# Two normalisation groups with GpSimd's reciprocal roots, and products without a reader in TensorE's waits

## What is computed

```python
for each of the two layers:
    h = _layernorm(x) * (1 + ca) + sa
    x = x + ga * attention(h)      # layer 0: convolutions, linear attention; layer 1: causal attention
    h = _layernorm(x) * (1 + cb) + sb
    x = x + gb * ffn(h)            # layer 0: 16 experts, top 4; layer 1: the stack below

def _L1_ffn_ref(x, ...):           # the windowed stack, DEPTH = 6, on 4 batches
    for i in range(DEPTH):
        x = attn_layer(shift_tokens(x), Wqkv[i], q_scale[i], k_scale[i], Wo[i]) + x
        x = ffn_layer(shift_tokens(x), ln_g[i], ln_b[i], W1[i], b1[i], W2[i], b2[i]) + x

def ffn_layer(x, g, bln, W1, b1, W2, b2):
    xn = layernorm(x) * g + bln
    a, gate = split(xn @ W1 + b1)  # 341 columns each
    return a * gelu(gate) @ W2 + b2
```

## Time and profile before

| what | value |
|---|---|
| median of 3 runs | 2385.68 us (2383.3 to 2389.93) |
| the profiled execution | 2394.28 us |
| its span, first to last instruction | 2392.7 us |
| PE busy | 2209.9 us (92%) |
| DVE, ACT, POOL busy | 1786.4, 1730.1, 1238.2 us |
| mean granted TensorE clock | 0.963 of full speed |

### The profile page before, as it was taken

One profiled execution on the slowest core, in us unless ns is written; L12 is line 12 of the kernel. 1 busy time (PEld: TensorE's weight loads), 2 busy tenths in 40 slices (PEclk: granted clock), 3 DMA queues, 4 the chain that ended last, 5 costly groups with the idle time before them and its releaser, 6 DMA issues.

```text
span 2392.7 us, 82108 instructions
## 1 busy us (share of the span) xinstructions
PE 2209.9 (92%) x33332; PEld 1573.3 (66%) x33332; DVE 1786.4 (75%) x3567; ACT 1730.1 (72%) x3982; POOL 1238.2 (52%) x2002
## 2 busy tenths in 40 slices
PE   6799679999976799999999999999999999999986
PEld 3478358888855566666766666666666676666662
DVE  3477377777777778888888888888888888888851
ACT  2255468888855578888888887887877888878870
POOL 0177010000000677777777777777777777776750
PEclk9899889999997899999999999999999999999996
DMA  2000022211102111112211111111111221111010
GB/s 89 10 1 2 2 96 76 80 64 70 71 2 82 28 51 53 49 49 60 58 51 51 45 53 53 51 47 55 53 51 51 56 61 45 58 53 54 25 40 22
DMA packets 40968, 117.74 MB, mean 49 GB/s; under 512 B 7953, under 2 KB 13393, under 8 KB 37777
## 3 DMA queue, kind: packets, MB, share of 16 engines
q1 hardware_dynamic: 40592, 112.49, 15.9%
HBM read 50.48 MB, written 2.23 MB: 22 GB/s over the span
## 4 chain that ended last, share of the span: by engine, by line
PE 50%; DVE 8%; ACT 5%; issue 3%; POOL 1%; DMA 0%; ACTq 0%; SPq 0%; POOLq 0%; DVEq 0%
PE w_psP L1784 13%; PE w_psT L1793 7%; PE w_psF L1728 7%; PE w_psS L1811 6%; PE w_psO L1840 6%; PE w_psF L1750 4%; PE w_psF L1754 3%; PE w_psT L1822 3%; ACT w_pb L1892 2%; DVE w_nrm L1957 2%; PE w_psS L1802 2%; ACT w_kT L1884 1%; DVE w_psP L1950 1%; DVE w_bb L1949 1%; DVE w_ab L1952 1%
## 5 line engine op out<-in xcount | busy, mean ns | idle before, releaser
L2054 POOL TENSOR_TENSOR w_ab<-w_ab,w_nrm 128x512 f32<-128x512 f32 x384 | 396.4, 1054 | 8.4 <-POOL w_nrm L84 8.4
L1892 ACT ACTIVATE w_pb<-w_psS,w_mx 128x64 f32<-128x64 f32 x1536 | 350.7, 347 | 2.6 <-PE w_psT L1822 1.0
L1784 PE MATMUL w_psP<-w_hi,w_xh 128*128 128x512 f32 x576 | 319.7, 555 | 33.5 <-DVE w_ab L1952 19.2
L2070 POOL TENSOR_TENSOR w_pb<-w_pb,w_sm 128x512 f32<-128x512 f32 x192 | 200.5, 1044 | 222.4 <-DVE w_sm L1970 222.4
L1957 DVE TENSOR_REDUCE w_nrm<-w_sq 128x8 f32<-128x512 f32 x384 | 251.9, 672 | 66.1 <-ACT w_sq L1867 66.1
L2046 POOL TENSOR_TENSOR w_ab<-w_ab,w_bb 128x512 f32<-128x512 f32 x192 | 245.5, 1279 | 87.3 <-DVE w_bb L1945 81.9
L1867 ACT ACTIVATE w_sq<-w_psP 128x512 f32<-128x512 f32 x384 | 235.6, 614 | 74.3 <-PE w_psP L1784 41.3
L1793 PE MATMUL w_psT<-tables_all,w_ab 128*128 128x128 f32 x1536 | 241.4, 280 | 7.3 <-POOL w_ab L2054 1.9
L1197 DVE TENSOR_TENSOR e_glo<-e_hh,e_ghi 128x512 fp32r<-128x512 f32 x256 | 169.5, 686 | 92.9 <-ACT e_ghi L1151 92.8
L1784 PE MATMUL w_psP<-w_lo,w_xh 128*128 128x512 f32 x576 | 229.5, 398 | 0.0
L1784 PE MATMUL w_psP<-w_hi,w_xl 128*128 128x512 f32 x576 | 229.1, 398 | 0.0
(11 more groups left out here) (294 smaller groups left out, 5387.0 us busy)
## 6 DMA issues: line engine op xcount, KB each, us to landing
X<-tables_layer SPq DMA_DIRECT2D x48, 384.0 KB, 3.7
X<-w_v SPq DMA_DIRECT2D x48, 384.0 KB, 3.6
e_gb<-gate_rows SPq DMA_DIRECT2D x16, 1024.0 KB, 4.8
e_raw<-in_w_moe SPq DMA_DIRECT2D x32, 256.0 KB, 5.2
w_raw<-in_w_qkv SPq DMA_DIRECT2D x20, 384.0 KB, 4.0
X<-tables_layer SPq DMA_DIRECT2D x48, 128.0 KB, 3.9
w_o<-in_w_o SPq DMA_DIRECT2D x6, 512.0 KB, 5.6
w_xs<-H SPq DMA_DIRECT2D x24, 128.0 KB, 2.2
```

The source lines that it names most:

```text
L1784: last = pe.matmul(psP[u % 2][:, :], x[r % 2][:, tt], w[:, layer % 2, ww], start=(n == 0), stop=(n == len(terms) - 1))
L1892: last = act.activation(pb[k % 2][:, n, :], psS[:, j, KEYS * q:KEYS * (q + 1)], ACT.Exp, bias=mx[:, n:n + 1])
L2054: pool.tensor_tensor(a, a, nrm[k // 2][:, 1, 8 * (i % 8):8 * (i % 8) + 8].unsqueeze(2).to_broadcast([128, 8, DH]), ALU.mult).then_inc(s["n ...
L2070: pool.tensor_tensor(p, p, sm[k % 2][:, :].unsqueeze(2).to_broadcast([128, PAIRS, KEYS]), ALU.mult).then_inc(s["pn"], 1)
```

## The change

It adds a helper `keep_busy`, which issues float32 products whose result nobody reads, and calls it in three places: in `adaln`, 4 products of 512 columns between the psX and the back transposes, into the bank `psB[3]`; in the first round, one product of 256 columns into `psF` ahead of each of the 24 units P and V, before their waits; in the last round's tail, 3 products ahead of `tr`, 5 ahead of `back`, one ahead of each of the other seven matmul steps, into `psP[0]`. Second, `adaln` takes statistics and aggregates in two groups of two batches; the roots and the shift of the first group are worked out by GpSimd (`rsqrt_simple` with 12 operations, and two for the shift), those of the second by VectorE, whose shift falls away.

```diff
--- before.py
+++ after.py
@@ -232,7 +232,7 @@
 
     nc = c.nc
     c.passed = c.sem("passed", keep=True)
-    c.adaln_sems = [c.sem("n_s_" + k, keep=True) for k in ("tr", "yn_act", "yn_dve", "back", "rs", "dve")]
+    c.adaln_sems = [c.sem("n_s_" + k, keep=True) for k in ("tr", "yn_act", "yn_dve", "back", "rs", "dve", "pool")]
     c.mods = c.sb("mods", [D, 2, 6, NB], keep=True)
     c.ident_bf = c.sb("ident_bf", [D, D], BF16, keep=True)
     c.band_bf = c.sb("band_bf", [D, 2, 256], BF16, keep=True)
@@ -294,6 +294,13 @@
             ch.link(dve.tensor_copy(c.band_bf[:, :, :], c.band[:, :, :]))
 
 
+def keep_busy(pe, bank, weights, moving, count):
+
+
+    for _ in range(count):
+        pe.matmul(bank, weights, moving, start=True, stop=True, skip_group_check=True)
+
+
 def adaln(c, layer, part, loads=None, yn=None):
 
 
@@ -307,7 +314,8 @@
     shift = c.sb(n + "shift", [128, NT])
     psX = [c.ps(n + f"psX{b}") for b in range(NB)]
     psB = [c.ps(n + f"psB{b}") for b in range(NB)]
-    s_tr, s_yn_act, s_yn_dve, s_bk, s_rs, s_ch = c.adaln_sems
+    s_tr, s_yn_act, s_yn_dve, s_bk, s_rs, s_ch, s_pool = c.adaln_sems
+    early, late = slice(0, NT // 2), slice(NT // 2, NT)
     call = 2 * layer + part
     gain = lambda b: c.mods[:, layer, 3 * part + 1, b:b + 1]
     add = lambda b: c.mods[:, layer, 3 * part, b:b + 1]
@@ -324,6 +332,7 @@
                     at = b * N + 128 * t
                     last = pe.transpose(psX[b][:, 128 * t:128 * t + 128], c.X[:, at:at + 128], c.ident[:, :])
                 last.then_inc(s_tr, 1)
+            keep_busy(pe, psB[3][:, :], c.ident[:, :], c.X[:, 0:N], 4)
             for b in (0, 2, 1, 3):
                 if b < 2:
                     pe.wait_ge(s_yn_act, call * 2 + b + 1)
@@ -349,17 +358,16 @@
         @block.vector
         def _(dve):
             ch = Chain(dve, s_ch, 2 * NT + 9, call)
-            for b in range(NB):
-                dve.wait_ge(s_tr, call * NB + b + 1)
-                for t in range(TILES):
-                    mark = ch.inc(dve.bn_stats(stats[:, b * TILES + t, :], psX[b][:, 128 * t:128 * t + 128]))
-            ch.wait(mark)
-            for k in range(NT):
-                mark = ch.inc(dve.bn_aggr(mv[:, k, :], stats[:, k, :]))
-            ch.wait(mark)
-            rsqrt(dve, ch, rs[:, 0, :], mv[:, :, 1], rs[:, 1, :], rs[:, 2, :], 1e-5, ALU.add)
-            dve.scalar_tensor_tensor(out=shift[:, :], in0=mv[:, :, 0], scalar=-1.0, in1=rs[:, 0, :], op0=ALU.mult,
-                                     op1=ALU.mult).then_inc(s_rs, 1)
+            for half in range(2):
+                for b in range(2 * half, 2 * half + 2):
+                    dve.wait_ge(s_tr, call * NB + b + 1)
+                    for t in range(TILES):
+                        mark = ch.inc(dve.bn_stats(stats[:, b * TILES + t, :], psX[b][:, 128 * t:128 * t + 128]))
+                ch.wait(mark)
+                for k in range(2 * TILES * half, 2 * TILES * (half + 1)):
+                    mark = ch.inc(dve.bn_aggr(mv[:, k, :], stats[:, k, :]))
+                ch.wait(mark)
+            rsqrt(dve, ch, rs[:, 0, late], mv[:, late, 1], rs[:, 1, late], rs[:, 2, late], 1e-5, ALU.add)
             for b in range(2, NB):
                 for t in range(TILES):
                     k = b * TILES + t
@@ -369,6 +377,15 @@
             for b in range(2, NB):
                 dve.wait_ge(s_bk, call * NB + 2 * (b - 2) + 2)
                 dve.tensor_scalar(c.H[:, b * N:(b + 1) * N], psB[b][:, :], gain(b), add(b), ALU.mult, ALU.add)
+            ch.end()
+
+        @block.gpsimd
+        def _(pool):
+            ch = Chain(pool, s_pool, 13, call)
+            pool.wait_ge(s_ch, call * (2 * NT + 9) + NT)
+            rsqrt_simple(pool, ch, rs[:, 0, early], mv[:, early, 1], rs[:, 1, early], rs[:, 2, early], 1e-5, ALU.add)
+            ch.link(pool.tensor_tensor(shift[:, early], mv[:, early, 0], rs[:, 0, early], ALU.mult))
+            pool.tensor_scalar(shift[:, early], shift[:, early], -1.0, None, ALU.mult).then_inc(s_rs, 1)
             ch.end()
 
 
@@ -1717,7 +1734,12 @@
                 sp.dma_start(out[:, b * N:(b + 1) * N], c.H[:, b * N:(b + 1) * N]).then_inc(s["xst"], 16)
             sp.wait_ge(s["xst"], 32 + 16 * NB)
 
+        WAITS = {"tr": 3, "back": 5, "g": 1, "a": 1, "w2": 1}
+
         def mm_tail(pe, f, r, layer):
+            if r == ROUNDS - 1 and f[:2] != "wo":
+                pe.wait_ge(s["vx"], ROUNDS * UV)
+                keep_busy(pe, psP[0][:, :], c.ident[:, :], w_1[:, 0:N], WAITS[f if f in WAITS else f[0]])
             if f[:2] == "wo":
                 half = int(f[2])
                 if half == 0:
@@ -1772,6 +1794,8 @@
                 if kind in "PV":
                     at = j if kind == "P" else 4 + j
                     u = 6 * k + at
+                    if r == 0:
+                        keep_busy(pe, psF[:, 0:N // 2], c.ident[:, :], c.H[:, 0:N // 2], 1)
                     if u == 0:
                         pe.wait_ge(s["wl"], layer * NB + 6 if layer else 1)
                         pe.wait_ge(s["xl"], r + 1)
```

## The result

The changed kernel took 2371.72 us (median of 4 runs, 2370.91 to 2375.8), the one before beside it 2387.38 (4 runs, 2383.3 to 2389.93): ratio 0.9941, 95% interval 0.9929 to 0.9954, 15.7 us faster. The forecast was 2373.7, 12.0 us less than before. The profiled execution after took 2370.91 us, its span is 2369.3.

What follows compares the result with a forecast made beforehand. TensorE, busy 92% of the span, bounds the kernel; in the tail each step waits for the previous one, at half clock. Terms -8.4 - 4.8 + 1.2 = -12.0 us take the median 2385.68 to 2373.7 us, range 2366.5 to 2381.5.

Steps and rivals of the forecast that it cites:

- The last tail: Last round's tail: full clock speeds `back`, six gate and value steps and `w2`; 8.8 us less 0.4, term -8.4 us.
- I cost the singles at nothing: Last tail: single products of 0.89 us fit about 1.0 us of room; if not, seven cost 0.1 us each.
- The one lapse of the clock behind the longest silence: Last tail: the clock may fall once after the 1.7 us silence left ahead of `back`; 0.4 us taken off.
- The normalisations: Four `adaln` calls: earlier ScalarE start and back transposes at full pace; 4 x 1.2, term -4.8 us.
- I take 1.2 us a call: Saving assumed per `adaln` call, between bounds of 0.27 and 1.56 us, nearer the upper end.
- the second rival: Clock lapses after `back` and in `adaln` silences, transposes perhaps not counting as work; about -5 us, 2380.7 us, chance 0.12.
- The first round: First round: 24 products of 256 columns, partly exposed, against shorter waits of VectorE; term +1.2 us.
- I take four products exposed: First round: four of the 24 products delay their units, 4 x 0.44 = 1.8 us.
- a faster unit would take part of them away: First round: faster units shorten VectorE's first two waits for squares; 1.25 us at most, half counted.
- I count the same saving there: Whole kernel: the saving worked out on the profiled execution, 12.0 us, applied also to the median of the runs.
- First round exposed: Rival: all 24 first-round products lie on the path; up to 10.7 us instead of 1.2, 2383.2 us, chance 0.10.
- Slower, products overrunning at half clock: Rival: products overrun waits in tail, `adaln` and first round while the clock stays 0.50; +17.2, 2402.9 us, chance 0.04.

Runs made afterwards that it cites:

- no_first: The changed kernel without the 24 products of the first round; 2380.32 us, ratio 0.9956 to the kernel before.
- tail22: The changed kernel with four more products, three in the last tail but one and one ahead of the last `wo`; 2375.15 us, ratio 0.995.
- tail_transposes: The changed kernel with each product of the last tail replaced by seven 128 x 128 transposes; 2376.18 us, ratio 0.9958.
- tail_single: The changed kernel with one product ahead of `tr` and one ahead of `back` instead of three and five; 2378.78 us, ratio 0.9964.
- tail_double: The changed kernel with twice the products in the last tail; 2384.20 us, ratio 0.9993.
- first_only: The kernel before with the 24 products of the first round alone; 2388.99 us, ratio 1.0005.
- after_again: The changed kernel, unchanged, timed again beside the kernel before; 2378.75 us, ratio 0.9962.

## Why the prediction was right, step by step

- **The last tail, -8.4 us.** Measured -8.7 in all eight kernels with as many products, or transposes in their place, as the change has, by the steps as priced: 0.45 for `back`, 0.94 to 0.96 for g0 and a0, 5.49 - 2.84 = 2.65 for `w2`. "I cost the singles at nothing" held. The one lapse of the clock behind the longest silence, for which 0.4 us was taken off, did not come: 1.00 from `wo` to 2367 us in the profile after.
- **The normalisations, -4.8 us.** Mean of the calls in the eight kernels with groups and these products and nothing else changed ahead of them (all of after, its two repeats, no_first, tail22, tail_transposes, tail_single, tail_double): 50.70, that is 54.87 - 50.70 = 4.2 us. The start of ScalarE came 0.27 us earlier in the first two calls (7.91 to 7.64), 0.21 in the fourth, as worked out from GpSimd's chain in another stage: the 3.9 us of that chain became 3.91 here, on 8 columns (the sum 753.3 + 3.9 is 757.2, not 757.3). "I take 1.2 us a call" was a little high: it is 1.04. Of these 32 calls one had all back transposes at half pace, three all but the first three or four, and nine the second half or a part of it, so that the lapsing clock of the second rival does come, in a share of the calls. With all of them at full pace the fourth call saves 1.39 us (11.95 in tail_double against 13.34), near the bound of 1.56.
- **The first round, +1.2 us.** A little high: nine kernels with the products have 174.2 to 176.7 us, mean 175.1, five without have 174.4 to 175.5, mean 174.9. That is +0.3 us, less than the kernels of either kind differ among themselves. The two steps are seen in part. "I take four products exposed" (1.8 us) was low as a count, since 3.2 and 4.8 us of products stand on the chain of first_only and after, and high as a price, since about 1.3 us are lost between the two steps timed above. The step "a faster unit would take part of them away" was entered at 0.6 us, and about 1.1 us are won ahead of the products on the chain. VectorE's waits for squares say little of it: 21.1 us in the round before, 19.2 after, but 19.2 to 19.9 in the four others without the products.
- **The sum, -12.0 us.** The stretches give -8.7 - 4.2 + 0.3 = -12.6. That it comes so near is in part luck, since the terms missed by 0.3, 0.6 and 0.9 us in both directions. The medians gave -15.7, -9.3 and -9.0, and their intervals overlap. The first lay within the range but above what the edited code explains; "I count the same saving there" left out that two stretches which the change leaves alone vary by 6.5 and 7.3 us between executions. That the difference between the three medians comes from these alone is likely but was not shown, since only one execution of each was traced, and the two repeats ran on two chips. For the clock speaks that the slower executions of one kernel have the lower mean granted clock: the fastest of after_again took 2372.29 us at 0.980, the slowest 2380.55 at 0.975.
- **The rivals.** First round exposed: products do stand on the chain, but the loss that this rival priced (up to 10.7 us) is refuted by first_only. Slower, products overrunning at half clock: seen for two products in tail_single, where the clock came back at once; the price of overrunning at full clock is that of tail_double. That transposes do not count was refuted by tail_transposes.

## What to carry to other kernels

Where nothing but a chain of small steps runs, read the granted clock of that stretch: a gate step of the tail took 2.04 us at 0.50 and 1.10 at 1.00, and work without a reader in the waits of the chain bought that back. How much of it to put there has to be tried: one product in each long wait in place of three and five cost 2.3 us here, twice the products 7.75. Ask too whether that work ends up on the chain itself: in the first round the clock rose from 0.67 to 0.91 and nothing was left of it. Judge edits of a few us by the stretches they touch in several profiles, since untouched code moved by as much from one execution to the next.

## What the runs showed that was not expected

The same 496 matmul rows of one kernel took 25.50 us in one execution and 32.84 in another, with the clock at 1.00 and at 0.74. Transposes alone in the waits of the tail kept the clock at 1.00, with TensorE busy for 22.34 of 29.60 us. In the first round products stood on the chain for 3.2 us and more, and the round was not longer. And the stretch between the first two calls, in which TensorE was busy for 221 of 266 us in the profile after, became 6.4 us or more shorter by 23 products that nobody reads.
